# Routing of the last tiles of a fused attention and mixture-of-experts block: fewer VectorE operations, another order on TensorE, fewer idle matmuls

## What is computed

```python
h = concatenate([patches @ proj_w.T + proj_b + pos_embed, txt])      # [8, 164, 192]
h = h + attention(layernorm(h))
x = layernorm(h)
normed = x * rsqrt(mean(x**2) + 1e-6) * ln_w
logits = normed @ w_router                                           # 16 experts
probs = softmax(logits); expert = argmax(probs)
priority = cumsum(onehot(expert), axis=tokens)                       # rank of a token in its expert, per batch
keep = onehot * (priority <= 64)                                     # 64 tokens per expert and batch
routed = relu(normed @ wi[expert]) @ wo[expert]                      # for the kept tokens
out = h + x + max(probs) * where(kept, routed, normed)
```

## Time and profile before

| | |
|---|---|
| median of 3 runs | 377.38 us (376.38 to 377.46) |
| the profiled execution | 378.11 us, its span 376.3 us |
| TensorE matmul, busy | 338.9 us (90%), 2360 instructions |
| VectorE, busy | 220.6 us (59%), 556 instructions |
| ScalarE, busy | 126.1 us (34%), 433 instructions |
| GpSimd, busy | 169.0 us (45%), 181 instructions |
| mean granted TensorE clock | 0.962 |

### The profile page before, as it was taken

How to read it: one execution, slowest core, us unless ns; L and a number is a source line. 1 busy time by engine, 2 the same in 40 slices (tenths; PEclk the granted TensorE clock), 3 DMA queues, 4 the chain that set the end, 5 groups by cost and what they waited for, 6 DMA issues and landing times.

```text
span 376.3 us, 6812 instructions
## 1 busy us (share of the span) xinstructions
PE 338.9 (90%) x2360; PEld 308.9 (82%) x2360; DVE 220.6 (59%) x556; ACT 126.1 (34%) x433; POOL 169.0 (45%) x181
## 2 busy tenths in 40 slices
PE   5987699999899899899898998998859999999992
PEld 2866499899699799798897998997723999999991
DVE  2378638668669578587677978657485222222221
ACT  2055424644453445426345024539100111111110
POOL 3058474674663862954836203140751134433321
PEclk9699969999999999999999999999968999999997
DMA  7499999799799799898997999600222499999950
GB/s 226 151 410 332 214 207 212 203 194 213 210 200 236 198 188 271 169 195 251 174 210 187 291 209 241 148 0 2 107 95 71 108 288 276 258 250 264 270 150 17
DMA packets 20176, 74.29 MB, mean 197 GB/s; under 512 B 3388, under 2 KB 9021, under 8 KB 18874
## 3 DMA queue, kind: packets, MB, share of 16 engines
q0 software_dynamic: 7344, 30.57, 40.3%
q1 hardware_dynamic: 9898, 40.40, 36.6%
q10 hardware_dynamic: 2912, 3.04, 3.1%
HBM read 66.12 MB, written 9.25 MB: 200 GB/s over the span
## 4 chain that ended last, share of the span: by engine, by line
PE 44%; issue 19%; POOL 15%; DVE 9%; DMA 7%; ACT 4%; POOLq 1%; SPq 0%; DVEq 0%; ACTq 0%
PE bO L1190 19%; PE bE L1190 10%; PE bS L1190 6%; POOL AwA L390 5%; PE bJ L1190 5%; DMA wbuf<-in_wte 4%; POOL PA L416 4%; POOL wbuf L401 3%; POOL AwB L390 2%; DMA AwA<-in_patches 2%; ACT PA L552 2%; PE bT L1190 1%; DVE negmax L786 1%; POOL PB L416 1%; PE bT L1535 1%
## 5 line engine op out<-in xcount | busy, mean ns | idle before, releaser
L552 ACT ACTIVATE PA<-bS,negmax 128x128 f32<-128x128 f32 x96 | 33.9, 366 | 85.4 <-DVE negmax L786 85.4
L416 POOL TENSOR_TENSOR PA<-PA,rn 128x512 f32<-128x512 f32 x24 | 25.5, 1062 | 66.4 <-DVE rn L798 66.3
L390 POOL TENSOR_TENSOR AwA<-zT,w 96x512 f32<-96x512 f32 x45 | 53.4, 1515 | 3.3 <-ACT zT L534 3.3
L1190 PE MATMUL bJ<-wo_sb,oTA 128*128 128x192 f32 x288 | 52.1, 331 | 0.0
L1190 PEld LDWEIGHTS bS<-zT,AwA 96*128 96x128 f32 x384 | 48.4, 198 | 1.2
L1190 PE MATMUL bS<-zT,AwA 96*128 96x128 f32 x384 | 48.4, 281 | 0.0
L1190 PEld LDWEIGHTS bJ<-wo_sb,oTA 128*128 128x128 f32 x288 | 47.2, 193 | 0.0
L1190 PE MATMUL bO<-PA,wx 96*128 96x112 f32 x384 | 45.4, 275 | 0.5 <-DVE PA L1163 0.5
L1190 PEld LDWEIGHTS bO<-PA,wx 96*128 96x128 f32 x384 | 44.9, 192 | 0.7 <-DVE PA L1163 0.7
L463 POOL DMA_INDIRECT out<-PA,yrow x16 | 15.0, 940 | 58.7 <-DVE PA L1179 58.7
L683 ACT ACTIVATE AwA<-bO 128x448 f32<-128x448 f32 x16 | 8.7, 543 | 82.6 <-PE bO L1190 74.1
(11 more groups left out here) (248 smaller groups left out, 697.2 us busy)
## 6 DMA issues: line engine op xcount, KB each, us to landing
wbuf<-in_wte POOLq DMA_DIRECT2D x20, 1344.0 KB, 12.9
wx<-in_wi SPq DMA_DIRECT2D x16, 576.0 KB
wx<-in_wo SPq DMA_DIRECT2D x16, 576.0 KB
wx<-in_wte SPq DMA_DIRECT2D x6, 1344.0 KB, 8.5
dispatched<-zeros SPq DMA_DIRECT2D x7, 675.5 KB, 10.6
wbuf<-in_wte SPq DMA_DIRECT2D x2, 1344.0 KB, 11.4
AwA<-dispatched ACTq DMA_DIRECT2D x14, 168.9 KB
wo_sb<-in_wo_attn SPq DMA_DIRECT2D x1, 1728.0 KB, 6.7
```

Of the source, the lines that this page charges most:

```text
L390: nc.gpsimd.tensor_tensor(o, zT[:, k, ss].unsqueeze(1).to_broadcast(list(o.shape)), w2[:, k, hs].unsqueeze(2).to_broadcast(list(o.shape)), ...
L416: nc.gpsimd.tensor_tensor(t, t, q.unsqueeze(2).to_broadcast(list(t.shape)), ALU.mult).then_inc(p_ready, 1)
L552: last = nc.scalar.activation(PA[:, h, :], bank[:, j * SA:(j + 1) * SA], ACT.Exp, bias=negmax[:, h:h + 1], accum_out=lsum[:, h:h + 1])
L1190: return nc.tensor.matmul(o, l, r, start=start, stop=stop, skip_group_check=True)
```

## The change

Six things are done:

1. VectorE, first stage: `routed(0)` and `exponents` are issued ahead of `row_scales(0)` and `base_factors(0)`; `keep` no longer makes `kept` and `drop` in three operations: one operation (`homes`) makes `drop` from `lidx`, and the mask is worked in where the address is summed (`(u - BIG) * kp`). `kept` is computed for all slots at once at the very end. `probability(B)` moves from ahead of `place(B)` to just before its last operation.
2. `newton` takes three operations, not four.
3. `place(1)` has one operation less: the term `shift` is made at the end of `place(0)`.
4. The `norm` rows of slots 9 and 10 are written by ScalarE in `bases`, with `nmc` from `base_factors`, as for the others; `norms` is gone. GpSimd's scatters wait for `cen_ready` throughout.
5. The exponentials of slots 9 and 10 are made on ScalarE one slot at a time from the logits less their maximum, with the row scale as the instruction's scale and the sum taken by its accumulator (`slot_exp`). VectorE's product and its reduction for these slots are gone.
6. TensorE: `project(LAST, 12, 14)` and then `expert_rank(0)` run ahead of `value(LAST, 3)`; the remaining four matmuls of the projection follow it. `stay_warm(bJ, 34)` becomes `stay_warm(bJ, 26)`.

ScalarE issues three slots' `norm` and `base` ahead of `o_copy(LAST, 3)`, not four, and `lx_exp` ahead of all.

```diff
@@ gpsimd
             for j in range(n0, SLOTS):
-                pool.wait_ge(norm_ready, j - n0 + 1)
+                pool.wait_ge(cen_ready, j + 1)
                 pool.wait_ge(base_ready, j + 1)
                 scatter(j)
@@ scalar, bases
-                    if g == 0:
-                        nc.scalar.activation(norm[:, k, :], H[:, ORD[k], :], ACT.Identity, bias=nmc[:, k:k + 1],
-                                             scale=rsq[:, 1, k:k + 1]).then_inc(cen_ready, 1)
+                    nc.scalar.activation(norm[:, k, :], H[:, ORD[k], :], ACT.Identity, bias=nmc[:, k:k + 1],
+                                         scale=rsq[:, 1, k:k + 1]).then_inc(cen_ready, 1)
...
+            def slot_exp(k):
+
+                act.wait_ge(le_ready, 3)
+                act.wait_ge(basepar_ready, 1 + k - GROUPS[0][1] + 1)
+                nc.scalar.activation(lx[:, k, :], lg[:, k, :], ACT.Exp, scale=rsq[:, 1, k:k + 1],
+                                     accum_out=lsm[:, k:k + 1]).then_inc(lx_ready, 1)
...
             nt_slot(5, 8, bS[0])
-            bases(0, 0, 2)
-            lx_exp(0)
-            bases(0, 2, 4)
+            lx_exp()
+            bases(0, 0, 3)
             o_copy(LAST, 3)
-            bases(0, 4)
+            bases(0, 3)
             nt_slot(6, 9, bS[0])
             bases(1)
             nt_slot(7, 10, bO[1])
-            lx_exp(1)
+            slot_exp(9)
+            slot_exp(10)
             bases(2)
@@ vector, newton
                 link(nc.vector.tensor_tensor(t, y, y, ALU.mult))
-                link(nc.vector.tensor_tensor(t, t, x, ALU.mult))
-                link(nc.vector.tensor_scalar(t, t, -0.5, 1.5, ALU.mult, ALU.add))
-                link(nc.vector.tensor_tensor(y, y, t, ALU.mult))
+                link(nc.vector.scalar_tensor_tensor(t, t, -0.5, x, ALU.mult, ALU.mult))
+                link(nc.vector.scalar_tensor_tensor(y, t, 1.5, y, ALU.add, ALU.mult))
@@ vector, probability, homes, keep
             def probability(B):
-                dve.wait_ge(lx_ready, B + 1)
-                link(nc.vector.tensor_reduce(part(lsm, B), part(lx, B), X, ALU.add))
+                if B:
+                    dve.wait_ge(lx_ready, 3)
+                else:
+                    dve.wait_ge(lx_ready, 1)
+                    link(nc.vector.tensor_reduce(part(lsm, B), part(lx, B), X, ALU.add))
                 nc.vector.reciprocal(pay[:, STAGE[B][0]:STAGE[B][1], D_RP], part(lsm, B)).then_inc(rp_ready, 1)
+
+            def homes(B):
+
+                link(nc.vector.tensor_scalar(part(drop, B), part(lidx, B), float(T), float(BIG + EXP * T), ALU.mult, ALU.add))
...
-                link(nc.vector.tensor_reduce(part(kept, B), part(kp, B), X, ALU.add))
-                link(nc.vector.tensor_scalar(part(drop, B), part(kept, B), -float(BIG), float(BIG + EXP * T), ALU.mult, ALU.add))
-                link(nc.vector.scalar_tensor_tensor(part(drop, B), part(lidx, B), float(T), part(drop, B), ALU.mult, ALU.add))
@@ vector, place
-                link(nc.vector.scalar_tensor_tensor(first[:, B, :], cst2[:, C_EM:C_EM + EXP], -float(T), first[:, B, :],
-                                                    ALU.mult, ALU.add))
+                if B:
+                    link(nc.vector.tensor_tensor(first[:, 1, :], first[:, 1, :], shift[:, :], ALU.add))
+                else:
+                    link(nc.vector.scalar_tensor_tensor(first[:, 0, :], cst2[:, C_EM:C_EM + EXP], -float(T), first[:, 0, :],
+                                                        ALU.mult, ALU.add))
...
                 if B:
-                    link(nc.vector.tensor_tensor(first[:, 1, :], first[:, 1, :], first[:, 0, :], ALU.subtract))
...
-                link(nc.vector.tensor_tensor(u, u, part(kp, B), ALU.mult))
+                link(nc.vector.scalar_tensor_tensor(u, u, -float(BIG), part(kp, B), ALU.add, ALU.mult))
                 link(nc.vector.tensor_reduce(part(posF, B), u, X, ALU.add))
+                probability(B)
                 nc.vector.tensor_tensor(part(posI, B), part(drop, B), part(posF, B), ALU.add).then_inc(pos_ready, 1)
+                if not B:
+                    link(nc.vector.scalar_tensor_tensor(shift[:, :], cst2[:, C_EM:C_EM + EXP], -float(T), first[:, 0, :],
+                                                        ALU.mult, ALU.subtract))
@@ vector, order
-            row_scales(0)
-            base_factors(0)
...
             routed(0)
-            exponents(0)
+            row_scales(0)
+            exponents()
+            base_factors(0)
             keep(0)
-            probability(0)
+            homes(0)
             place(0)
...
             variance(1)
-            norms(1)
+            row_scales(1)
+            base_factors(1)
...
             routed(1)
-            norms(2)
-            exponents(1)
+            row_scales(2)
             keep(1)
-            probability(1)
+            base_factors(2)
+            homes(1)
             place(1)
...
+            link(nc.vector.tensor_reduce(kept[:, :], kp[:, :, :], X, ALU.add))
             link(nc.vector.scalar_tensor_tensor(dropF[:, :], kept[:, :], float(BIG), pay[:, :, D_ROW], ALU.mult, ALU.add))
@@ tensor
             text_rank(1).then_inc(rank_ready, 1)
-            value(LAST, 3)
+            project(LAST, 12, 14)
             pe.wait_ge(t_used, TPB * NBATCH)
             pe.wait_ge(tl_used, 5 * NBATCH)
             expert_rank(0)
-            project(LAST, 12, WCH)
+            value(LAST, 3)
+            project(LAST, 14, WCH)
...
-            stay_warm(bJ, 34)
+            stay_warm(bJ, 26)
```

More of the change, by code:

```diff
@@ L157, in program @@
         oneX = sb("oneX", [128, EXP])
-        capB = sb("capB", [128, EXP])
+        capB, shift = sb("capB", [128, EXP]), sb("shift", [128, EXP])
         bex, beC = sb("bex", [128, 2 * EXP]), sb("beC", [128, 1])
@@ L631, in nt_slot, with lx_exp @@
                                      ACT.Copy).then_inc(nT_ready, 1)
-            def lx_exp(B):
-                k0, k1 = STAGE[B]
-                act.wait_ge(le_ready, 2 * B + 2)
+            def lx_exp():
+                k0, k1 = STAGE[0]
+                act.wait_ge(le_ready, 2)
                 nc.scalar.activation(lx[:, k0:k1, :], lg[:, k0:k1, :], ACT.Exp).then_inc(lx_ready, 1)
+            def slot_exp(k):
[3 more added lines that the diff above has]
+                                     accum_out=lsm[:, k:k + 1]).then_inc(lx_ready, 1)
             b = LAST - 1
@@ L975, in base_factors @@
                 k0, k1 = GROUPS[g]
-                if g == 0:
-                    nc.vector.scalar_tensor_tensor(nmc[:, k0:k1], fmv[:, k0:k1, 0], -1.0, rsq[:, 1, k0:k1], ALU.mult, ALU.mult)
+                nc.vector.scalar_tensor_tensor(nmc[:, k0:k1], fmv[:, k0:k1, 0], -1.0, rsq[:, 1, k0:k1], ALU.mult, ALU.mult)
                 link(nc.vector.tensor_scalar(rsq1[:, k0:k1], rsq[:, 0, k0:k1], 1.0, None, ALU.add))
@@ L980, in base_factors @@
                                                ALU.mult).then_inc(basepar_ready, 1)
[L982 to L988, removed]
             def part(t, B):
@@ L1008, in routed, with exponents @@
                 nc.vector.tensor_tensor(part(oh, B), em, part(lidx, B).unsqueeze(2).to_broadcast(bc), ALU.is_equal).then_inc(oh_ready, 1)
-            def exponents(B):
-                (k0, k1), s = STAGE[B], STAGE[B][1] - STAGE[B][0]
-                nc.vector.tensor_tensor(part(lg, B), part(lg, B), rsq[:, 1, k0:k1].unsqueeze(2).to_broadcast([128, s, EXP]),
+            def exponents():
+                (k0, k1), s = STAGE[0], STAGE[0][1] - STAGE[0][0]
+                nc.vector.tensor_tensor(part(lg, 0), part(lg, 0), rsq[:, 1, k0:k1].unsqueeze(2).to_broadcast([128, s, EXP]),
                                         ALU.mult).then_inc(le_ready, 1)
             def probability(B):
-                dve.wait_ge(lx_ready, B + 1)
-                link(nc.vector.tensor_reduce(part(lsm, B), part(lx, B), X, ALU.add))
+                if B:
[3 more added lines that the diff above has]
+                    link(nc.vector.tensor_reduce(part(lsm, B), part(lx, B), X, ALU.add))
                 nc.vector.reciprocal(pay[:, STAGE[B][0]:STAGE[B][1], D_RP], part(lsm, B)).then_inc(rp_ready, 1)
+            def homes(B):
+                link(nc.vector.tensor_scalar(part(drop, B), part(lidx, B), float(T), float(BIG + EXP * T), ALU.mult, ALU.add))
             def keep(B):
```

## The result

| | before | after |
|---|---|---|
| median | 376.94 us (4 runs, 376.38 to 377.46) | 372.17 us (4 runs, 371.76 to 374.59) |
| profiled execution, its span | 378.11, 376.3 | 372.14, 370.4 |
| VectorE instructions | 556 | 546 |
| mean granted clock | 0.962 | 0.976 |

The ratio is 0.9877, with a 95% interval of 0.9834 to 0.9919: 4.8 us by the medians, anything from 3.1 to 6.3 by the interval. The forecast was 372.8. The profiled executions differ by 6.0, more than the medians, and why is part of what follows. All medians in this text leave out two executions in a slower state of the core, one of before (382.98) and one of `e3_before_order` (378.48).

What follows compares the result with a forecast made beforehand. Bound: TensorE's expert loop, its first matmul held by 34 idle matmuls, the gather next. Gains 1.35 + 1.5 (earlier start) + 1.72 (eight fewer) = 4.57 us; 377.38 - 4.57 = 372.8 us, own range 371.8 to 374.0, 8-in-10 range 371.0 to 375.2.

Steps and rivals of the forecast that it cites:

- The bound: Ahead of the expert loop: idle matmuls, not gathered data, release the first real matmul; the gather is late next.
- Part 1: First nine tiles (`place(0)`): text copy and everything behind it come 1.35 us earlier, bounds 0.8 to 1.65.
- The step that names the order as what pays: First nine tiles: VectorE's early start is nearly worthless; TensorE's expert ranks ahead of the values are taken up 2.05 us earlier.
- Part 2: Last tile, one-hot to `posI` on VectorE: 23 operations instead of 29 save 1.46, say 1.5 us, bounds 1.0 to 1.8.
- The covers: Last tile: ScalarE's exponentials, norm and base stay covered by 1.1 us, GpSimd's queue ahead of the next scatter by 1.2.
- the rival case in which both last ones are stretched: GpSimd's last two scatters slowed by VectorE's products: 1.41 us more, sum 4.1 instead of 4.57; no chance of its own.
- Part 3: Idle matmuls ahead of the expert loop: 26 instead of 34 save eight at 0.215, 1.72 us.
- The sum: Whole kernel: 2.85 us earlier start of the idle matmuls plus 1.72 for eight fewer, 4.57 us.
- The clock stays high: Rival: idle matmuls run at the high clock, the gather decides; 5.9 us less, 371.5 us; chance 0.12.
- it would be low at the row's start: Start of the idle matmuls: low clock likely, after 3.8 us of TensorE nearly idle; 26 then take 8.0 us.
- Shortening not passed on: Rival, first nine tiles or last tile: one lost, 374.2 us, chance 0.08; both lost, 375.7 us, chance 0.08.
- The low clock reaches into the loop: Rival: expert blocks run at 1.2 GHz; one stretch 376.2 us, chance 0.03; two 379.6 us, slower, chance 0.03.

Runs made afterwards that it cites:

- e3_before_order: Kernel before with only TensorE's new order (two projection matmuls and the expert ranks ahead of the last values), 34 idle matmuls kept; 373.66 us, ratio 0.9917.
- e1: Kernel before with 26 idle matmuls ahead of the expert loop instead of 34, nothing else; 375.49 us against 376.40, ratio 0.9971.
- e5: Changed kernel with 20 idle matmuls instead of 26; 371.11 us, ratio 0.9857.
- f1: Changed kernel with the first stage's probability back in the wait for the expert ranks and `shift` behind the text copy; 372.16 us, ratio 0.9891.
- e4: Changed kernel with TensorE's old order (last values, then expert ranks, then six projection matmuls); 375.74 us.
- a1_after: Changed kernel measured again, unaltered, on another chip; 372.23 us against 376.22, ratio 0.9876.
- e2: Changed kernel with 34 idle matmuls, as before, instead of 26; 373.33 us, ratio 0.9905.
- e6: Changed kernel with 8 idle matmuls instead of 26; 375.41 us.
- f2: Changed kernel with first-stage probability back in the wait for the ranks, `shift` behind the text copy, and 20 idle matmuls; 371.38 us, ratio 0.9846.
- f3: Changed kernel with `nmc` and the norm rows of slots 9 and 10 as before, on VectorE; 372.88 us.
- e7: Changed kernel with 19 instead of 10 matmuls in the row ahead of the block table, to keep the clock up; 373.07 us.
- f4_order_26: Kernel before with two edits only, TensorE's new order and 26 idle matmuls; 373.26 us, ratio 0.9903.

## Why the prediction was right

- **The bound.** That the idle matmuls let the transpose go, and that the gather is next by under a microsecond, is shown by `e1` (gain, no wait) and `e5`. There the transpose gained 0.45 and then waited 0.54, where the forecast's 286.3 and 285.35 left 0.95: the gather is nearer than forecast.
- **Part 1: 1.35 forecast, 1.47 measured** (text copy 9.88 to 8.41). The ranks were taken up 2.07 sooner (2.05), the added operations cost 0.60 (`capI` to copy 3.53 in place of 2.93; `f1`, without them, is back at 2.93). That the ranks came at the forecast time is in part luck: the mask began 3.62 after the logits where the forecast had 3.82 (256.75), since TensorE began the rank matmuls sooner, and from mask to `capI` it took 1.26 instead of 1.08. The step that names the order as what pays is shown by `e3` (1.57 alone) and `e4`.
- **Part 2: 1.46 forecast, 1.33 measured** (one-hot to `posI`, 6.19 to 4.86). One-hot to keep: 1.06 (1.04 forecast). Keep to `capI`: 0.16 (0.32), the one term off, by the 0.38 of `drop` above, which the earlier trace rows couldn't show. `capI` to `posI`: 0.11 (0.10). The covers held: the reciprocal waited for no exponential, and the next scatter started 0.81 us behind the end of `posI`, as before. The last scatter kept its length (2.36), so the rival case in which both last ones are stretched didn't come.
- **Part 3: 1.72 forecast.** The profiles show 2.68, the medians 0.9 (`e1`) and 1.1 (`a1_after` less `e2`: 373.33 - 372.23, across chips). The interval of `e1` (0.3 to 1.9) holds 1.72. The term rests on both rows being equally long at 1.2 GHz. Where they are, it is exact (`e3` and after, both 2.91 us: 8.76 and 7.04). Between before and after they weren't: after's clock was back 1.95 us sooner, which is worth about 0.97, all of the excess. Why the medians give less than 1.72 is open.
- **The sum.** 4.57 forecast; 5.51 between the profiles up to the first transpose, of which 0.96 is the clock; 4.8 and 4.0 by the medians. That 372.8 lies so near the measured time owes something to its base: 377.38, the median of three runs, is about 1.0 above the 376.2 to 376.4 of the larger groups. From those, 4.57 less would have been 371.6 to 371.8, against 372.2 measured.
- **The rivals.** *The clock stays high* happened for a whole row in no profile without a bridge. The forecast that it would be low at the row's start is only half right: in six profiles (`e1`, `e4`, `e6`, `f1`, `f2`, `f3`) it was at 1.00 there and fell 0.2 to 0.9 us into the row, for 3.4 us. In `e7`, at 1.00 throughout, the row took the 5.6 forecast for it. *Shortening not passed on*: not seen. *The low clock reaches into the loop*: real, and priced by `e6`, but not with 26. What none of the rivals had is that the clock can fall behind the old order's idle gap ahead of the text projection (`e4`, 1.6 us). How often that happened in the kernel before isn't known: its one profile didn't have it.

## What to carry to other kernels

Where one engine's serial chain of small operations and another's block of matmuls both lie between two points, look at which instruction the chain waits for, and issue that ahead of the block: moving one block of matmuls gave more (1.57 us in the profile of `e3`) than ten operations saved on VectorE (1.33 less 0.1). Move a short operation into a wait that exists rather than behind it. Idle matmuls that keep the clock up are a cost like any other as soon as they end later than the data, and here a count that lets the data come last by a little had the lowest medians, and in `e5` the least scatter; far fewer cost more than they saved.

## What the hardware showed that was not expected

- A gap of 2.20 us in TensorE's work was followed by a fall of the granted clock to 1.2 GHz (`e4_after_old_order`), one of 1.51 us in the same place wasn't (before). Each is one profile.
- The same row of 26 idle matmuls was at the low level for 2.9 us in two profiles, 3.4 in four and 6.0 in `f4_order_26`, and took 7.04, 7.30 and 8.57 us; 34 took 8.76 to 9.72. Each of these lengths is 0.215 us for each matmul plus half of the time at the low level, within 0.02 us.
- A VectorE operation on 128x2 elements took 0.36 to 0.39 us in one place in every profile with the changed last stage, ending with a scatter of GpSimd, and 0.15 when a wide one stood ahead of it and the scatter had ended.
- GpSimd's last scatter took 2.36 us again (2.39 in the earlier trace rows), VectorE's wide products starting 0.99 us ahead of it. The one before it took 0.99, though the products began 0.30 us after its start. In `e7_bridge`, where they began 0.53 after the start of the last, that took 0.93. So it isn't its being the last that makes it long; in all fourteen profiles a scatter is stretched only when it starts beside the products.
